# Attention batches of a graph network: the store of sums in four pieces, paced by the gathers

## The reference, cut to what matters

```
xw   = (x @ W).reshape(n, 4, 32)
al_s = einsum('nhf,hf->nh', xw, a_src);  al_d = einsum('nhf,hf->nh', xw, a_dst)
e    = leaky_relu(al_s[src] + al_d[dst], 0.2)
m    = segment_max(e, dst);  ee = exp(e - m[dst]);  den = segment_sum(ee, dst)
out  = segment_sum((ee / den[dst])[:, :, None] * xw[src], dst) + b
```

## Time and profile before

| | |
|---|---|
| median of 3 runs | 7106.29 us (7104.17 to 7130.43) |
| the profiled execution, its span (the page gives no other time of its own) | 9134.2 us |
| TensorE matmul busy | 6058.7 us (66%) |
| TensorE weight load busy | 4168.5 us (46%) |
| VectorE busy | 4902.9 us (54%) |
| ScalarE busy | 2128.7 us (23%) |
| GpSimd busy | 3226.6 us (35%) |
| mean granted TensorE clock | 0.798 of full speed |

### The profile page before, as it was taken

The page is one execution under the profiler, slowest core; times in us unless marked ns, Lnnn a source line. Parts: engine busy times, 40 slices in busy tenths (PEclk is TensorE's granted clock), DMA queues, the critical chain, the costliest instruction groups (busy, mean ns, idle before and its releaser), DMA issues.

```text
span 9134.2 us, 96786 instructions
## 1 busy us (share of the span) xinstructions
PE 6058.7 (66%) x33473; PEld 4168.5 (46%) x33473; DVE 4902.9 (54%) x15778; ACT 2128.7 (23%) x3520; POOL 3226.6 (35%) x3274
## 2 busy tenths in 40 slices
PE   7999899898882565656665556516666655556663
PEld 6999677686662233333333333313333333333332
DVE  8999568584344444444444444535444444444445
ACT  3555454456441011111111111111111111111111
POOL 1221000000005444444444444264444444444432
PEclk9999999999996677777777777657777777777776
DMA  4332767789942233333333333222333333333332
GB/s 144 128 130 120 263 229 263 238 270 236 227 91 59 67 80 80 77 76 77 81 81 81 81 81 81 61 50 74 77 75 78 81 81 81 81 81 80 80 73 78
DMA packets 1103555, 1021.75 MB, mean 112 GB/s; under 512 B 467063, under 2 KB 957709, under 8 KB 1098870
## 3 DMA queue, kind: packets, MB, share of 16 engines
q1 hardware_dynamic: 998150, 790.99, 30.4%
q0 software_dynamic: 104976, 225.47, 10.2%
HBM read 569.77 MB, written 346.75 MB: 100 GB/s over the span
## 4 chain that ended last, share of the span: by engine, by line
DVE 28%; another core or an unknown queue 28%; issue 7%; PE 7%; ACT 1%; DMA 0%; DVEq 0%; SPq 0%; ACTq 0%
DVE arena L2039 10%; PE PS L1397 4%; DVE arena L2026 4%; DVE arena L2017 4%; DVE arena L2002 1%; DVE arena L2007 1%; DVE arena L2009 1%; DVE arena L2006 1%; DVE arena L2010 1%; DVE arena L2004 1%; PE PS L1306 1%; DVE arena L2001 1%; DVE arena L2049 1%; PE PS L1384 0%
## 5 line engine op out<-in xcount | busy, mean ns | idle before, releaser
L827 POOL DMA_INDIRECT arena<-table,arena x2944 | 2796.1, 950 | 2829.6 <-PE PS L1384 1960.3
L1397 PE MATMUL PS<-X,arena 128*128 128x396 bf16 x5952 | 1664.7, 409 | 1677.6 <-issue 1676.7
L1397 PEld LDWEIGHTS PS<-X,arena 128*128 128x128 bf16 x5952 | 647.4, 111 | 2618.4 <-issue 2400.7
L2049 DVE TENSOR_REDUCE arena<-PS 128x132 f32<-128x396 f32 x192 | 108.9, 567 | 2851.1 <-remote 2811.3
L1030 ACT ACTIVATE arena<-PS 128x396 f32<-128x396 f32 (+1 forms) x1078 | 528.4, 490 | 3836.2 <-PE PS L1384 3814.5
L1174 PE MATMUL PS<-count_pieces,node_halves 128*128 128x512 f32 (+1 forms) x4704 | 1086.1, 388 | 71.0 <-DVE count_pieces L1777 36.4
L2039 DVE TENSOR_SCALAR arena<-shift 128x128 bf16<-128x128 bf16 x9408 | 995.4, 187 | 176.5 <-issue 173.1
L1174 PEld LDWEIGHTS PS<-count_pieces,node_halves 128*128 128x128 f32 x4704 | 858.7, 189 | 242.5 <-issue 37.5
L1384 PE MATMUL PS<-arena 128*128 128x132 f32 x6272 | 823.1, 285 | 2.9 <-DVE arena L2026 2.6
L1113 PE MATMUL PS<-arena 128*128 128x49 bf16 x7936 | 803.3, 278 | 25.0 <-DVE arena L1615 22.6
L1113 PEld LDWEIGHTS PS<-arena 128*128 128x128 bf16 x7936 | 775.9, 150 | 55.6 <-issue 46.3
(11 more groups left out here) (372 smaller groups left out, 4952.7 us busy)
## 6 DMA issues: line engine op xcount, KB each, us to landing
arena<-counts SPq DMA_DIRECT2D x315, 896.0 KB, 4.7
segment_sums<-arena SPq DMA_DIRECT2D x96, 2176.0 KB
counts<-arena SPq DMA_DIRECT2D x31, 3136.0 KB, 9.4
arena<-table,arena POOLq DMA_INDIRECT x2944
vec<-edge_rows SPq DMA_DIRECT2D x192, 64.0 KB
arena<-counts SPq DMA_DIRECT2D x21, 448.0 KB, 3.3
table<-arena SPq DMA_DIRECT2D x2, 3332.0 KB
arena<-table SPq DMA_DIRECT2D x2, 3332.0 KB
```

The source lines that it names most:

```text
L827: g_.indirect_dma_start(out=ring[n % RING][:, i, :], out_offset=None, in_=table_d[j][:, :], in_offset=bass.IndirectOffsetOnAxis(ap=other[: ...
L1397: last = t_.matmul(PS[:, 6 + t, 0:SPLIT * SW], spots[t][:, b, :], parts_of(b).rearrange("p t f -> p (t f)"), start=(b == 0), stop=(b == NB ...
```

## The change

The store of batch k is cut in four pieces of eight tiles, for all batches with k + 3 < 49. The first goes out as the whole store did before. The three others wait on a new semaphore `gather_turn`, which GpSimd increments when it has issued 8, 16 and 24 gathers of a batch k >= 3; SP's batch k waits for the increments of GpSimd's batch k + 3. Batches 46 and 47 store in one piece, batch 48 in three, as before. The counts of pieces that others wait for are worked out anew. The semaphore `scores_taken` is dropped; TensorE's `turn_scores(n)` waits for `logits` instead, which comes later in the same `score`.

```diff
         PIECES = ((0, 12), (12, 24), (24, BT))
+        TURNS = ((0, 8), (8, 16), (16, 24), (24, BT))
+
+        def pieces(k):
+            return TURNS if k + RING < BATCHES else PIECES if k == BATCHES - 1 else ((0, BT),)
+
+        def stores_ahead(n, b):
+            return sum(len(pieces(x % BATCHES)) for x in range(b, n, 2))
 
         def stores(j, b):
-            return done_batches(j, b) + sum((len(PIECES) - 1) * ((BATCHES * (x + 1) - 1) % 2 == b) for x in range(j + 1))
-
-        def stores_ahead(n, b):
-            return (n + 1 - b) // 2 + (stores(0, b) - done_batches(0, b) if n >= BATCHES else 0)
+            return stores_ahead(BATCHES * (j + 1), b)
...
-                    lo = PIECES[-1][0] if k == BATCHES - 1 else 0
-                    sp.dma_start(by_tile[:, lo:BT, :], out_rows[:, lo:BT, :]).then_inc(s[f"sums_stored{n % 2}"], 16)
+                    for p, (lo, hi) in enumerate(pieces(k)):
+                        if k == BATCHES - 1 and p < len(PIECES) - 1:
+                            continue
+                        if k + RING < BATCHES and p > 0:
+                            sp.wait_ge(s["gather_turn"], (len(TURNS) - 1) * (n - j * RING) + p)
+                        sp.dma_start(by_tile[:, lo:hi, :], out_rows[:, lo:hi, :]).then_inc(s[f"sums_stored{n % 2}"], 16)
                     if k + 2 < BATCHES:
                         terms(k + 2)
                     if k + 3 < BATCHES:
...
                           .then_inc(s[f"rows_in_{n % RING}"], 16)
+                        if k >= RING and i + 1 in [lo for lo, hi in TURNS]:
+                            pool.sem_inc(s["gather_turn"])
...
-                need(pe, "scores_taken", n)
+                need(pe, "logits", n)
...
-                dve.sem_inc(s["scores_taken"])
```

More of the change, by code:

```diff
@@ L327, in gnn_kernel @@
                      "gru_gates", "gru_rz", "gru_pre", "gru_n", "gru_new", "gru_back", "gru_done",                      "group_in", "dve_chain", "low_hot", "row_stats", "low_copied0", "low_copied1", "fills_stored", "x_ready", "h_turned", "hT_ready", "xw_done",
-                     "table_ready", "table_stored", "bias_set", "first_rows", "first_stored", "rows_in_0", "rows_in_1",
-                     "rows_in_2", "terms_in0", "terms_in1", "scores_turned", "scores_taken", "logits", "weights",
+                     "table_ready", "table_stored", "gather_turn", "bias_set", "first_rows", "first_stored", "rows_in_0", "rows_in_1",
+                     "rows_in_2", "terms_in0", "terms_in1", "scores_turned", "logits", "weights",
                      "weights_turned", "tops_turned", "weights_in", "tops_in", "weighed", "hot_ready", "seg_sums", "sums_taken",
```

## The result

The changed kernel takes 7192.01 us (median of 4, 7188.32 to 7193.51) against 7107.01 us of the kernel before beside it (4 runs, 7104.17 to 7130.43): ratio 1.0115, 95% interval 1.0099 to 1.0131. It is slower, by 85 us. The forecast was 8516 us, 1410 us slower; the direction was right, the size some sixteen times too large.

A forecast was written before the change was run, and what follows sets the result against it. Timed runs bound by GpSimd's gathers, 37.5 us a batch; 45 intervals growing 14.7 us (661.5) plus 43.4 at the end make 704.9 per stage, twice 1410, on 7106: 8516 us, range 7850 to 8950.

The forecast's parts named there:

- The stall: TensorE's pick_rows in the first profile, 15 matmuls in 24 us; claimed little or nothing of it in timed runs.
- B: Rival: TensorE's stall is in the timed runs and stays, period 58.1 us; no change, 7106 us; chance 0.07, with D.
- C: Rival: the store's burst causes the stall in pick_rows, so the change is faster, 6563 us; chance 0.04.
- A: Rival: GpSimd's gathers are faster unrecorded, the 0.305 us between them belonging to the recording; 7867 us; chance 0.10.
- T0 = 37.5 us: GpSimd's time for a batch's 30 gathers at 1.25 us each, taken as the timed period before the change.
- The same event opens both: Last sums of batch n release its store and, 0.3 us later, GpSimd's gathers of batch n+3.
- S: Start of a batch's gathers on GpSimd, from which the prediction counts its times; 4510.96 in the first profile.
- The gate: SP's piece 3 waits for 24 gathers of batch n+3, 30.0 us, plus 0.1 us for the increment: S + 30.1.
- Rival D: The gate does not bite, GpSimd being far ahead; excluded in steady work; chance counted with B, 0.07.
- Behind the gate on SP: Last piece, terms, resets and sources follow the gate in order; sources landed 36.9 us after S.
- The tail: From VectorE's spot (L2035) through second row, transposes and sums to GpSimd's next first gather: 15.3 us.
- The end of an attention: After the start of batch 48's gathers: 105.1 us instead of 61.7, adding 43.4 us per stage.

The follow-up runs named there:

- second profile of before: The kernel before, unchanged, profiled again to see whether the 24 us stall of TensorE returns; 7160 us.
- the gate at the landing: Changed kernel without increments; only the last piece waits, for the landing of all 30 gathers of the batch being filled; 9279 us in one run.

## Why the prediction was wrong

*The stall.* "The timed runs have little or nothing of the stall and are bound in these 98 batches by GpSimd's gathers": right, shown by the second profile of before. Rivals B and C fell with it, and A too: the 0.305 us between gathers is there in profiles as long as the timed runs.

*T0 = 37.5 us.* Off by 1 to 2 us: 38.3 to 39.3 on average in the profiles without waits, since gathers get longer beside VectorE's score and, now and then, beside its tensor_scalars. In the first profile the score (4506.70 to 4513.45) fell into GpSimd's wait but for its last 2.5 us, and no gather took over 1.222 us.

*"The same event opens both."* True in the first profile and in the changed kernel, not in the kernel before as it is timed: there the sums of batch n are done 27 us ahead of S. It cost nothing in the sum, since a gate behind S takes that lead away before it costs anything; it does explain the ends of the attentions (below).

*The gate: "Piece 3 waits for 24 gathers of batch n+3: 24 x 1.25 = 30.0 us".* This is the step that failed. The increment behind gather 24 goes out when gather 12 ends: S + 14.7 (the median; 12 gathers begun in all 92 batches). I took an increment behind an instruction in the program for one behind its work. The trace of before could not show it, but I had bounded this term from neither side. With it 15.4 us earlier, the terms that follow give 52.2 - 15.4 = 36.8 us, which is below GpSimd's own time: no change but for the ends. Rival D was put aside by the same slip: the sums of n hold the first gather of batch n+3, but the increment behind its gather 8 was out up to 5.2 us before that gather, so the second piece hardly waits at all.

*Behind the gate on SP.* Right in kind and near in sum, since two sizes are off against each other: terms' issue 0.58 us (I took 2.0), resets 1.1, sources with their landing 4.3 (4539.47 to 4543.73; I took 3.0). Sources are used 21.1 us after S, thus 6.3 behind the gate (I had 6.8).

*The tail* from L2035 to the next gathers: 17.5 us, not 15.3. The transposes take 1.0 for 0.6 and the sums 9 to 10 us for 8.36, both after TensorE had stood idle for 7 us. The windows of the changed kernel (as the earlier trace rows) show the clock there:

```profile
4550.00:4552.00 2.00, 1.64 (x8) 1.48 (x9) 2.00 (x18) 0.00 (x0) 1.69 (x2) 0.50 0.31 70
4552.00:4561.00 9.00, 9.00 (x62) 8.67 (x60) 8.83 (x39) 4.68 (x10) 5.92 (x7) 0.80 0.25 54
```

It is 0.50 of full speed (1.2 GHz) with the transposes and 0.80 on average with the sums; the first profile of before had 1.00 in both (4559 to 4561 and 4560 to 4569). So the chain is 14.7 + 6.3 + 17.5 = 38.5 us, level with GpSimd's own 30 x (0.980 + 0.305) = 38.5: some waits appear, 919.9 - 897.2 = 22.7 us in the first profile of the changed kernel and 25.5 in its second.

*The end of an attention.* Forecast 43.4 us each; measured 28.5 and 26.7. This is the same slip once more: with sources at 21.1 instead of 36.9 the forecast's sum is 105.1 - 15.8 = 89.3, and less 61.7 it leaves 27.6. The mechanism held: paced stores make TensorE late against the gathers, and the lateness comes due when the gathers end. It makes over half of the 100 us.

*The rule of the Trainium skill* that the prediction weighed (DMA: Bandwidth & Descriptors, "Anatomy of one DMA — SWDGE (gpsimd) path"), that a wait is served on the issuing sequencer, held. On SP it put the loads behind the gate: in the batch above they start 0.05 us after the last piece. What I did not ask is the same question of GpSimd: what its sequencer has passed when an increment goes out.

## What to carry to other kernels

A semaphore increment that stood by itself behind an asynchronous instruction told how far the queue had been filled, not how far the work was; here that was 12 gathers. Where a gate must mean work, wait on what the data set, and measure where the gate opens before summing a chain behind it. When a profile's span is not the timed median, find the period that makes up the difference before anything is read from its waits. And ask what stands behind a wait on an in-order queue, not only what the transfer that waits is worth: of the 81 us in waits and ends here, moving the loads ahead of the wait took away 49, and the paced store kept 31.

## What was not expected of the hardware

GpSimd's increments ran 12 gathers ahead, in the changed kernel and with the increments moved (last piece at 14.7 and at 22.5 us, in all batches). Gathers of 0.944 us took up to 1.4 us on average at one place in the batch (the 28th in the changed kernel, 1.37 us), beside the scores on VectorE, with the copy or without; where scores and gathers hardly met, as with the gate at the landing, the mean was 0.947. Single gathers took 4.8 us beside a series of 49 tensor_scalars on VectorE, and 6.4 us where the score followed on it. And the first profile of before had a stall of TensorE that made it 2028 us longer than the median and 1895 us longer than the longest timed run (7239 us), and that nothing here explains.
